# Edge loop of a graph network: the hand-over of a batch's running maxima by copies of SyncE in place of small products of TensorE

## The reference

```
s     = leaky_relu(x_l[src] + x_r[dst] + e_attr @ W_e.T, 0.2)     # (edges, 4 heads, 64)
alpha = einsum('ehc,hc->eh', s, att)
amax  = segment_max(alpha, dst)
ex    = exp(alpha - amax[dst])
out   = segment_sum(ex / denom[dst] * x_l[src], dst)
```

## Time and profile before

| | |
|---|---|
| time, 3 runs | median 3181.06 us (3168.73 to 3182.11) |
| profiled execution: span | 3452.9 us (no other time of it was taken) |
| TensorE busy | 3048.3 us, 88% of the span |
| VectorE busy | 1834.2 us, 53% |
| ScalarE busy | 1508.7 us, 44% |
| GpSimd busy | 1189.9 us, 34% |
| mean granted clock of TensorE | 0.944 |
| DMA | 345.06 MB in 288628 packets |

### The profile page before, as it was taken

How to read it: one execution, slowest core, us unless ns; L and a number is a source line. 1 busy time by engine, 2 the same in 40 slices (tenths; PEclk the granted TensorE clock), 3 DMA queues, 4 the chain that set the end, 5 groups by cost and what they waited for, 6 DMA issues and landing times. The chain is left out here.

```text
span 3452.9 us, 50836 instructions
## 1 busy us (share of the span) xinstructions
PE 3048.3 (88%) x13612; PEld 2420.6 (70%) x13613; DVE 1834.2 (53%) x3643; ACT 1508.7 (44%) x4936; POOL 1189.9 (34%) x1152
## 2 busy tenths in 40 slices
PE   6678888788888888884999999999999999999999
PEld 5456656566565665563778877877787888888898
DVE  5566666666676666676754564374365435111103
ACT  2067666777667676775322322232231212222232
POOL 4556555565555655630310031030021001222210
PEclk9899899999999999997999999999999988999999
DMA  7556655555665655554211011100001032333361
GB/s 217 152 148 148 145 145 141 143 144 141 149 145 145 147 142 150 136 94 124 52 38 37 27 30 31 41 8 1 15 27 50 1 100 84 128 120 119 119 176 38
DMA packets 288628, 345.06 MB, mean 100 GB/s; under 512 B 155176, under 2 KB 213655, under 8 KB 284512
## 3 DMA queue, kind: packets, MB, share of 16 engines
q1 hardware_dynamic: 232813, 174.79, 19.1%
q0 software_dynamic: 53632, 157.89, 17.6%
q10 hardware_dynamic: 2064, 10.81, 1.0%
HBM read 298.03 MB, written 44.37 MB: 99 GB/s over the span
## 5 line engine op out<-in xcount | busy, mean ns | idle before, releaser
L1470 POOL DMA_INDIRECT a_g<-xl_d,a_ix x480 | 468.1, 975 | 311.6 <-issue 116.0
L1504 PE MATMUL b_pM<-b_m,b_oh 128*112 128x281 f32 x1680 | 513.6, 451 | 28.5 <-DVE g_acc L1644 22.5
L1599 ACT ACTIVATE b_m<-a_g,c_pcx 128x64 f32<-128x64 f32 x1856 | 460.4, 334 | 33.6 <-issue 33.6
L1504 PEld LDWEIGHTS b_pM<-b_m,b_oh 128*112 128x112 f32 x1680 | 327.6, 200 | 156.7 <-issue 69.0
L1470 POOL DMA_INDIRECT XS<-xl_d,a_ix x344 | 333.3, 969 | 216.5 <-issue 91.1
L1637 DVE SCALAR_TENSOR_TENSOR a_r<-a_pS,g_attx 128x528 f32<-128x528 f32 x420 | 286.6, 699 | 198.4 <-remote 91.6
L1599 ACT ACTIVATE b_m<-XS,c_pcx 128x64 f32<-128x64 f32 x1424 | 351.5, 333 | 14.3 <-issue 14.2
L2286 ACT ACTIVATE f_hid<-f_pH,f_b 128x256 f32<-128x256 f32 (+3 forms) x360 | 161.9, 451 | 423.0 <-PE f_pH L2180 409.9
L450 PE MATMUL m_pH<-m_h,m_w 128*128 128x313 f32 (+1 forms) x1280 | 342.3, 426 | 4.5 <-DVE m_h L612 4.5
L125 POOL TENSOR_TENSOR m_rstd<-m_ve,m_mhalf 125x5 f32<-125x5 f32 x41 | 48.0, 1170 | 801.5 <-DVE m_ve L111 801.5
L1497 PE MATMUL a_pS<-g_xr,a_lt 128*128 x840 | 237.1, 406 | 97.8 <-ACT a_pS L1581 60.8
(11 more groups left out here) (413 smaller groups left out, 4629.2 us busy)
## 6 DMA issues: line engine op xcount, KB each, us to landing
a_db<-dl_d SPq DMA_DIRECT2D x212, 224.0 KB
f_w<-in_ffn_W1p SPq DMA_DIRECT2D x16, 1024.0 KB
wide_w<-in_ffn_W1p SPq DMA_DIRECT2D x16, 1024.0 KB
m_w<-in_mix_W SPq DMA_DIRECT2D x8, 1024.0 KB
f_w<-in_ffn_W2p SPq DMA_DIRECT2D x8, 1024.0 KB
a_g<-xl_d,a_ix POOLq DMA_INDIRECT x480
a_lt<-eat_d SPq DMA_DIRECT2D x214, 32.0 KB
eat_d<-a_stage SPq DMA_DIRECT2D x15, 448.0 KB
```

What stands on the lines that cost most here:

```text
L1470: p.indirect_dma_start(out=gathered(t)[:, j, :], out_offset=None, in_=xl_d, in_offset=bass.IndirectOffsetOnAxis(ap=IX[:, t // BSTEPS, n:n ...
L1504: ins = pe.matmul(pM[0:WN, h, 0:MW], OH[:, b, j, :], M[:, b, j, :], start=(j == 2 * h), stop=(j == 2 * h + 1))
L1599: ins = a.activation(m[:, j, part], gathered(ts)[:, j, part], ACT.Copy, scale=of[:, first + j, h, 0:1])
```

## The change

The six small products go. In tau 0 SyncE, as the last thing of its slot, waits for `c_scan` and copies the last column of the forward scan (116 partitions, one element each) into a row `c_row` in SBUF, and the first column of the backward scan into its second row. VectorE puts the carried values into the row's four free places with a copy of four elements, waits for its own copy, and scans the row out of SBUF. In tau 1 SyncE waits for `c_rowscan` and copies the two scanned rows back to columns in `c_init`, from which VectorE scans again without a copy of its own. `c_rows` and `c_cols` now count 32 a batch. The tiles `c_one` and `c_low` go (the low value comes from `a_alpha`'s initial filling, now LOW where it was 0), and TensorE's wait on `c_pcx` moves to the transposes in tau 3.

```
@@ sync
+ tau, odd, n = chain_of(i, t)
+ par = 1 if odd else 0
+ if tau == 0:
+     sp.wait_ge(s["c_scan"], n)
+     sp.dma_start(RW[0:1, 0, 1:CP + 1], FB[:, 0, TE - 1:TE]).then_inc(s["c_rows"], 16)
+     sp.dma_start(RW[0:1, 1, 0:CP], FB[:, 1, 0:1]).then_inc(s["c_rows"], 16)
+ elif tau == 1:
+     sp.wait_ge(s["c_rowscan"], n)
+     for d in range(2):
+         sp.dma_start(IN[:, d:d + 1], ST[0:1, par, d, d:d + CP]).then_inc(s["c_cols"], 16)
...
@@ tensor
+ wait(pe, "c_pcx", n, -1)        # tau 3
- if tau == 1:
-     pe.wait_ge(s["c_rowscan"], n)
-     for d in range(2):
-         ins = pe.matmul(pY[0:CP, 240 + d:241 + d], ST[0:1, par, d, d:d + CP], one[:, :], start=True, stop=True)
-     ins.then_inc(s["c_cols"], 1)
...
- if tau == 0:
-     pe.wait_ge(s["c_scan"], n)
-     wait(pe, "c_pcx", n, -1)
-     rows = [by_item(pY[0:1, d * CP:(d + 1) * CP]) for d in range(2)]
-     eye = by_item(ident[0:CP, 0:CP])[:, :, 0:BI]
-     pe.matmul(rows[0][:, :, 1:], FB[:, 0, TE - 1:TE], eye, start=True, stop=True)
-     pe.matmul(rows[0][:, :, 0], one[:, :], by_item(ST[0:1, 1 - par, 0, 0:CP])[:, :, BI], start=True, stop=True)
-     pe.matmul(rows[1][:, :, BI], one[:, :], low[:, :], start=True, stop=True)
-     pe.matmul(rows[1][:, :, 0:BI], FB[:, 1, 0:1], eye, start=True, stop=True).then_inc(s["c_rows"], 1)
...
@@ vector
- v.memset(AX_[:, :, :, :], 0.0)
+ v.memset(AX_[:, :, :, :], LOW)
...
- v.wait_ge(s["c_cols"], n)
- v.tensor_copy(IN[:, :], pY[0:CP, 240:242]).then_inc(s["c_init"], 1)
- v.wait_ge(s["c_init"], n)
- v.sem_inc(s["c_seen"], 1)
+ v.wait_ge(s["c_cols"], 32 * n)
...
- v.wait_ge(s["c_rows"], n)
+ v.wait_ge(s["c_rows"], 32 * n)
+ v.tensor_copy(by_item(RW[0:1, 0, 0:CP])[:, :, 0], by_item(ST[0:1, 1 - par, 0, 0:CP])[:, :, BI]).then_inc(s["c_carried"], 1)
+ v.wait_ge(s["c_carried"], n)
...
-                pY[0:1, d * CP:(d + 1) * CP][:, ::way], LOW, ALU.add, ALU.max)
+                RW[0:1, d, 0:CP][:, ::way], LOW, ALU.add, ALU.max)
```

More of the change, by code:

```diff
@@ L1306, in graph_attention @@
                 IN = sb("c_init", [CP, 2])
+                RW = sb("c_row", [1, 2, CP + 1])
                 PCX = sb("c_pcx", [TE, 2, BI, GH, 2])
                 fade = sb("c_fade", [1, GH])
-                one = sb("c_one", [1, 1])
-                low = sb("c_low", [1, GH])
                 minus = sb("c_minus", [1, GH])
@@ L1405, in _ @@
                     nodes_ahead, attributes_ahead = 3, 4
-                    sp.wait_ge(s["a_const"], 7)
+                    sp.wait_ge(s["a_const"], 5)
                     def staged(i):
@@ L1438, in _ @@
                     sp.wait_ge(s["s_staged"], 32 * ROUNDS)
+                    sp.wait_ge(s["c_rows"], 32 * NB)
+                    sp.wait_ge(s["c_cols"], 32 * NB)
                     for k in range(2):
@@ L1567, in _ @@
                     ins.then_inc(s["a_opened"], 1)
-                    pe.wait_ge(s["a_const"], 7)
+                    pe.wait_ge(s["a_const"], 5)
                     rounds(pe, slot)
@@ L1612, in _ @@
                     v.memset(ST[:, :, :, :], LOW)
-                    v.memset(AX_[:, :, :, :], 0.0)
+                    v.memset(AX_[:, :, :, :], LOW)
                     v.memset(BR[:, :, :, :], 0.0)
                     v.memset(ANY[:, :, :, :, :], LOW).then_inc(s["a_const"], 1)
-                    v.memset(one[:, :], 1.0).then_inc(s["a_const"], 1)
-                    v.memset(low[:, :], LOW).then_inc(s["a_const"], 1)
                     v.memset(minus[:, :], -1.0).then_inc(s["a_const"], 1)
-                    v.wait_ge(s["a_const"], 7)
+                    v.wait_ge(s["a_const"], 5)
                     flat = ACC[:, :, :].rearrange("p w m -> p (w m)")
```

## The result

The changed kernel takes 3216.69 us (median of 4 runs, 3213.09 to 3219.06), the kernel before, run beside it, 3180.36 us (4 runs). The ratio is 1.0127, with a 95% interval of 1.0105 to 1.0148: slower by 1.3%, 36 us between the medians and some 40 us by the ratio, where 3142 us was forecast. The profiled execution took 3218.27 us, its span is 3216.4 us. One thing has to be known ahead of any comparison: the kernel before takes about 3175 us on some chips and 3460 us on another, and its profile in the earlier trace rows, with a span of 3452.9 us and its waits on "remote", is by both of the second kind. The trace of the changed kernel is of the first. So a ratio is taken only between runs made side by side on one chip, and the two traces are compared only in what doesn't depend on the chip.

A forecast was written before the change was run, and what follows sets the result against it. Four edge-loop engines were within 10%, GpSimd's gathers the floor at 36.6 of 39.0 us a batch. Rows -1.01, columns -0.6, wait +0.3 gave -1.3 us, times 30 -39: 3142 us, range 3115 to 3165.

The forecast's parts named there:

- The step that failed: VectorE's wait for the row copies before the row scan: 0 to 4.15 us a batch, taken as 0.3.
- rival C: Edge loop: copies' round trips outlast their cover, sharing rings with `a_db` and gathers; +2.1 us a batch, 3244 us; chance 0.22.
- The bound of 5.7 us: Upper end for a row or column copy's leg, from the longest wait on the tile list; mean 2.4 us.
- The stretch by the profiler: The profiled span's 271.8 us above the median was put into the edge loop, as standstills stretched by the profiler.
- 39.0 us a batch: Edge loop's batch length without the profiler, scaled from 47.75 us by 1208/1480.
- D: Edge loop: standstills come from the small products, also unprofiled; -2.9 us a batch, 3094 us, or 3109 by GpSimd's floor; chance 0.10.
- The freed time: TensorE in the batch's two hand-over slots: 1.01 us from row products, 0.6 from column products; 1.6 a batch, 48 in all.
- rival B: Edge loop: nothing gained, as GpSimd's 36.6 us and VectorE's 11.05 us in two slots stand; 3172 us; chance 0.28.
- coupling of 2.4 us: Edge loop: batch of 39.0 us less GpSimd's floor of 36.6; 72 us in all, lost between engines.
- A: Edge loop: TensorE's time comes back in full, within the 72 us of coupling; 3142 us; chance 0.40.
- Columns hidden: Column copies before VectorE's rescan: 2.75 us covered by 3.2 us of other VectorE work, so no wait.
- SyncE's queue: The next slot's `a_db` load goes 3 us later behind the wait on `c_scan`; covered, no cost; SyncE issues 25 us of 39.

The follow-up runs named there:

- the version with one copy: Changed kernel with one copy of 116 pairs each way in place of two of single elements: 3184.22 us; with staging gathers three slots later too, 3157.47 us.
- the four kernels on that chip: Rows by TensorE, columns by copies: ratio 1.0012; the reverse: 0.9966; full change with row scan reading the previous batch's row: 0.9944; full change with staging later: 0.9953.
- rows a batch late: Full change, but the row scan reads the row copied a batch earlier and the wait stands before the rescan: 3182.67 us, ratio 1.0036 on a quick chip.

## Why the prediction was wrong

**The step that failed** is "So the wait is from 0 to 4.15 us, 0.85 at the mean; I take 0.3". Measured are 3.15 us a batch, about 1.4 and 4.9 in turn, the longest 6.0. So rival C was the case: the round trips got longer than their cover. Its sizes were not: it had 2.25 us for the rows and 1.45 for the columns, 3244 us in all; measured are 3.15 and next to nothing, 3217. Two things in the step were off.
- The leg. 1.90 us was read off the tile list, one copy alone. In the quiet batch the second of two copies took 2.94 us, and a single copy of pairs, 0.76 us earlier, 2.44 from its issue. The rest of that term was right: 0.03 us for the semaphore, 0.76 for the first issue (0.75 taken), 2.4 us of cover. The 2 us of the Trainium skill (DMA: Bandwidth & Descriptors, Anatomy of one DMA) is below both measured legs; that section gives it for DMAs on GpSimd's path, and these copies are SyncE's.
- The place. Every second batch's copies go out two to three microseconds behind the two staging gathers, which GpSimd, up to three slots ahead, issues at the very time of the scans; there the leg is 6.61 us. I named the rings shared with `a_db` and the gathers in rival C, but averaged over the batch; the trace has SyncE's packets in one queue with `a_db`, q1, and GpSimd's in another, q0, so it is the engines that the copies share with the gathers. That the staging gathers are the cause of the long leg is shown: moved by three slots, they take the wait from 58.5 to 4.8 us, and 27 us with it, and the copies' packets start late only in the batches in which 8 KB packets are under way. The Trainium skill (DMA: Bandwidth & Descriptors, Queues, rings and completion order) says that a DMA's semaphore increment lands only after every earlier write of the same DMA engine, across queues. That could act only behind the copy's last packet, where the version with one copy shows 1.18 us in place of 0.57; of its 4.1 us of added leg, 2.7 pass before the first packet. Why the packets start late, the engines' order of work or something else, isn't shown.

**The bound of 5.7 us was a wait and no leg.** It was the prediction's upper end and rival C's evidence, and it came from the earlier trace rows. In the trace of the kernel before GpSimd stands idle from 665.92, SyncE issues the list only at 668.95, and the gather starts at 671.67:

```profile
668.95 0.33 SPq L1415 DMA_DIRECT2D a_tix<-tl_d  x1
...
671.67 0.91 POOL L1456 DMA_INDIRECT a_stage<-in_gnn_eaT,a_tix  x1 [5.75 <-DMA a_tix<-tl_d]
```

That leg is 2.72 us. The mean of 2.4 is one of waits too. From 300 to 1446 us the legs of this list lie between 1.5 and 2.7 us, and none has an 8 KB packet beside it. So no row of the kernel before showed the 3.8 us that rival C's sum went by, and that its 5.7 came near the 6.61 measured is luck. What could be read there was the place: GpSimd's staging gathers go out in the slot ahead of the scans of every second batch.

**A price that no term held**: TensorE's clock. Behind the 5.16 us idle period it is 0.50 for eight passes, about 2 us in the round shown. Over the loop TensorE is busy for 70 us at that level in the changed kernel, for 25 us in the version with one copy and staging later, and for 22 us in the kernel before with its staging moved. Half of the difference, some 22 us, is what the clock costs, an estimate by the eight passes that take twice as long. That the same slot had a clock of 0.84 in the earlier trace rows, behind 3.12 us of idleness in the earlier trace rows, was there to be read; I priced it nowhere.

**The stretch by the profiler** was wrong, and with it the 39.0 us a batch: the profiled execution of the kernel before was longer than the timed ones for its chip and not for the profiler. Every profiled execution measured with its time has a span 1.5 to 2.0 us under it, on either kind of chip; the 272 us were another chip's. On a quick chip the batch of the kernel before with its staging moved is 37.77 us (start of its row scans, 145.2 to 1240.4 us, over 29). That the standstills aren't the price of the products was right; the experiments show it, and D falls: they were there in each of the four kernels on that chip, with or without products, and on a quick chip the kernel before with its staging moved has no wait on "remote" at all. What "remote" stands for stays open.

**The freed time** of the rows was sized right and turned into little; the 0.6 us of the columns have no measurement of their own. The sums run in one piece in the slot of the scans, so the 1.01 us came back:

```profile
1015.21 2.06 PE L1515 MATMUL b_pM<-b_m,b_oh 128*112 128x281 f32 x8
```

But with the waits nearly removed, the version with one copy is 37.53 us a batch long, (1235.8 - 147.4)/29, against 37.77 without the change: 0.24 us, of 1.6 freed. In whole runs it is 12 us (3157.47 against 3169.43), where 48 were to be freed and 39 gained. GpSimd's gathers stand close below, as rival B had it: in the timeline of the kernel with rows a batch late they go off every 1.25 us, eleven steps in 13.79, so 28 of them (35.1) and one of the two staging gathers of a round (1.3) take 36.4 us a batch. My coupling of 2.4 us was 1.4, 41 us in all: barely room for the forecast of 39, and most of it wasn't to be had even with next to no wait for the rows. What holds it there isn't shown. A's step "TensorE's time comes back in full" fails too, though it isn't what turned the sign.

```profile
1019.58 0.96 POOL L1481 DMA_INDIRECT XS<-xl_d,a_ix  x1 [0.31 <-issue]
...
1033.37 0.95 POOL L1481 DMA_INDIRECT XS<-xl_d,a_ix  x1 [0.30 <-issue]
```

**Columns hidden**: right in the changed kernel (three waits of 1.6 us in all from 160 to 1350), for a reason I hadn't seen; alone they cost 45.8 us of VectorE's time, and what TensorE gets back from them doesn't show (ratio 1.002).

**SyncE's queue, `a_db`, `c_pcx`, the scan out of SBUF**: as said. In the changed kernel no wait on `a_db` is left in the list; the row scan takes 387 ns in place of 366 (median).

**The sum**, in terms as measured, a round of two batches: the wait 2 x 3.15 = 6.3 and the clock 22/15 = 1.5 against 3.2 us freed, +4.6 or 69 us over 15 rounds; measured are 36 and 43. The rest, some 30 us, did not cost time. GpSimd, 8.82 of 11.84 us busy in the long slot, works ahead during the wait, which may be why; no run shows it.

## What to carry to other kernels

A hand-over by a small copy costs its leg at that very place in the schedule, so look for what else is issued in the few microseconds before it: a mean leg over all places is no bound. Take a leg from the issue to the reader and never from a wait, which also holds the time in which nothing had been issued yet. Moving a burst away is cheap and can be worth more than the change itself (27 us here, and both kernels are beaten, by 0.4% and 1.8%). Before a span is set against a time, ask whether both come from the same chip, and read the time freed on one engine against the next engine's own floor.

## What the runs showed of the hardware

- The same kernel takes 3171 to 3181 us on some chips and 3460 on another. The surplus lies in the edge loop, in standstills of several engines at once: the kernel before takes 47.3 us a batch there (its row scans start from 159.3 to 1531.9 us, over 29), where the quick chips show 37.8 with the staging moved; the dense part is the same within 4 us. What makes the chips differ isn't shown.
- A copy of 116 single elements from SBUF to SBUF took 2.9 us from its issue to its reader, one of 116 pairs 2.4, and behind two staging gathers 6.6.
- The packets of a small copy start late while large ones of another queue are under way. With 112 packets of 8 KB under way its first packet started 4.1 us after the issue in place of 1.4, the last of them 1.0 us later in place of 0.3, and the reader 1.2 us after that in place of 0.6 (medians of 14 and 16 batches of the kernel with one copy each way).
- A copy of 116 pieces ended in 4 packets of 4 bytes and one of 128 pieces in 16, and the kernels took the same time (ratios 0.996 and 0.9956).
- A wait need not vanish with its cause: with the row wait taken out, two others of 50 to 60 us came up in the same rounds.
